# Normalisations on both sides of the linear attention in batches of four tiles, and the fifth unit's final product ahead of one

## The reference, cut to what matters

```python
h = h + soft_moe(layernorm(h))                # its last product is added to h
x = layernorm(h)                              # normalised once
g = ln(x) * ln1_w + ln1_b                     # and again
k, v = g @ Wk_a.T, g @ Wv_a.T
sr = sigmoid(g @ Wr_a.T)
y = bi_wkv(decay / T, first / T, k, v)        # (ef*af + eb*ab + ec*v) / (ef*bf + eb*bb + ec)
x = x + sr * y @ Wo_a.T
g = ln(x) * ln2_w + ln2_b
kf = square(relu(g @ Wk_f.T))
x = x + sigmoid(g @ Wr_f.T) * (kf @ Wv_f.T)
```

## Time and profile before

| | |
|---|---|
| median of 3 runs | 1508.24 us (1503.82 to 1509.28) |
| profiled execution | 1508.46 us, span 1506.7 us |
| mean granted clock of TensorE | 0.952 |
| busy: TensorE matmul, weight load | 1324.3 us (88%), 763.3 us (51%) |
| busy: DVE, ACT, POOL | 911.4 us (60%), 673.4 us (45%), 553.1 us (37%) |

### The profile page before, as it was taken

The page is one execution under the profiler, slowest core; times in us unless marked ns, Lnnn a source line. Parts: engine busy times, 40 slices in busy tenths (PEclk is TensorE's granted clock), DMA queues, the critical chain, the costliest instruction groups (busy, mean ns, idle before and its releaser), DMA issues.

```text
span 1506.7 us, 18440 instructions
## 1 busy us (share of the span) xinstructions
PE 1324.3 (88%) x6684; PEld 763.3 (51%) x6684; DVE 911.4 (60%) x1509; ACT 673.4 (45%) x1210; POOL 553.1 (37%) x399
## 2 busy tenths in 40 slices
PE   7978889898989867389988869979999999999998
PEld 6634445454545434254433444558756668444444
DVE  4789999999999999862100168846446614121022
ACT  4776767677777744152100027631452241313311
POOL 1477898988989887300000010012044202000000
PEclk9989999999999999779999979999999999899999
DMA  6404051422414040437999920000000001020101
GB/s 205 172 2 171 13 162 35 138 76 96 128 45 171 12 161 0 187 129 265 399 391 400 328 70 1 1 0 1 22 17 2 1 1 38 0 110 14 37 0 33
DMA packets 38773, 151.96 MB, mean 101 GB/s; under 512 B 10364, under 2 KB 14587, under 8 KB 33948
## 3 DMA queue, kind: packets, MB, share of 16 engines
q1 hardware_dynamic: 34588, 149.21, 27.5%
q10 hardware_dynamic: 4096, 1.58, 0.4%
HBM read 147.56 MB, written 1.63 MB: 99 GB/s over the span
## 4 chain that ended last, share of the span: by engine, by line
PE 51%; DVE 20%; issue 11%; ACT 6%; POOL 6%; DMA 5%; SPq 1%; ACTq 0%; DVEq 0%; POOLq 0%
PE ps L1915 49%; DVE arena L1508 7%; DVE arena L1497 5%; DMA arena<-in_e_b 4%; POOL arena L824 4%; ACT arena L926 2%; ACT ps L1037 1%; DVE stats L1392 1%; DVE arena L1798 1%; PE ps L1924 1%; SPq L636 1%; ACT arena L931 1%; DVE arena L1517 1%; POOL arena L835 1%; POOL arena L839 1%
## 5 line engine op out<-in xcount | busy, mean ns | idle before, releaser
L1915 PE MATMUL ps<-arena 64*32 64x384 f32 (+17 forms) x5236 | 948.6, 416 | 100.2 <-ACT arena L926 22.4
L1915 PEld LDWEIGHTS ps<-arena 64*32 64x32 f32 (+15 forms) x5236 | 537.3, 154 | 483.0 <-issue 288.6
L824 POOL TENSOR_TENSOR arena<-arena 128x784 f32<-128x784 f32 x192 | 367.4, 1927 | 95.3 <-DVE arena L1508 94.7
L1915 PE MATMUL ps<-arena,ident 128*128 128x392 f32 x900 | 348.3, 515 | 50.9 <-POOL arena L824 42.7
L1508 DVE TENSOR_TENSOR_SCAN arena<-ps,arena 128x784 f32<-128x784 f32 x192 | 341.0, 1776 | 2.4 <-ACT ps L1037 2.4
L1915 PEld LDWEIGHTS ps<-arena,ident 128*128 128x128 f32 x900 | 169.1, 195 | 199.2 <-POOL arena L824 74.2
L1037 ACT ACTIVATE ps<-arena 128x384 f32<-128x384 f32 x384 | 207.9, 575 | 115.8 <-DVE arena L1508 115.1
L926 ACT ACTIVATE arena<-ps 128x392 f32<-128x392 f32 (+9 forms) x269 | 126.7, 489 | 284.7 <-PE ps L1915 203.4
L926 ACT ACTIVATE arena<-ps,arena 128x392 f32<-128x392 f32 (+2 forms) x191 | 103.4, 602 | 229.6 <-PE ps L1915 144.8
L1497 DVE TENSOR_TENSOR arena<-ps,arena 128x784 f32<-128x784 f32 x192 | 182.7, 952 | 6.0 <-ACT ps L1063 4.8
L1661 DVE COPY arena<-ps 128x384 f32<-128x384 f32 x32 | 16.3, 552 | 152.5 <-PE ps L2169 152.5
(11 more groups left out here) (201 smaller groups left out, 854.6 us busy)
## 6 DMA issues: line engine op xcount, KB each, us to landing
arena<-in_e_w SPq DMA_DIRECT2D x32, 2304.0 KB
arena<-bc_rows SPq DMA_DIRECT2D x128, 392.0 KB, 4.7
arena<-in_patches SPq DMA_DIRECT2D x4, 1176.0 KB, 7.5
arena<-comb_rows SPq DMA_DIRECT2D x1, 3136.0 KB, 10.7
arena<-in_mlp_w SPq DMA_DIRECT2D x5, 576.0 KB, 4.3
arena<-arena ACTq DMA_DIRECT2D x128, 12.0 KB, 8.2
arena<-in_mlp_w SPq DMA_DIRECT2D x5, 384.0 KB, 3.4
arena<-in_mlp_w SPq DMA_DIRECT2D x10, 192.0 KB, 3.9
```

The costliest lines, as they stand in the source:

```text
L824: pool.tensor_tensor(pair(hbuf[:, at % SLOTS, :]), pair(hbuf[:, at % SLOTS, :]), c_all[:, n:n + 2, :], ALU.mult).then_inc(times_c, 1)
L1915: return pe.matmul(dst, lhsT, rhs, start=first, stop=last)
```

## The change

The eight tiles of the first half are normalised in two batches of four at both borders, with the turns, the copies and the products split to match: one batch feeds one quarter. At the first border the second half (batch of eight, `mixed(range(4, 8))`) moves behind `front(0)`, and its turn behind `arguments(0)`. At the second border `final(4)` stands ahead of `attended`. The banks are given out anew. The amount of matrix and activation work is the same; DVE gets one more chain of small instructions at each border.

```diff
-        s_mix = items("mix", 8, "dve")
+        s_mix = stage("mix", "dve")
+        plan(s_mix, 8, (0, 1, 2, 3, 5, 6, 7, 0), "dve")
...
-        plan(s_xaT, 4, (0, 1, 2, 3), "act")
-        plan(s_kvr, 6, (0, 1, 2, 3), "act")
-        plan(s_xaT, 4, (4, 5, 6, 7), "act")
+        plan(s_xaT, 2, (1, 2), "act")
+        plan(s_kvr, 3, (3, 1, 2), "act")
+        plan(s_xaT, 2, (3, 1), "act")
+        plan(s_kvr, 3, (2, 3, 1), "act")
...
+            if t == 0:
+                plan(s_xaT, 4, (5, 6, 7, 0), "act")
...
-        plan(s_xbT, 4, (0, 1, 2, 3), "act")
-        plan(s_rf, 4, (4, 5, 6, 7), "act")
-        plan(s_kf, 12, range(8), "act")
+        plan(s_xbT, 2, (2, 3), "act")
+        plan(s_rf, 2, (4, 0), "act")
+        plan(s_kf, 6, (1, 7, 2, 3, 4, 0), "act")
+        plan(s_xbT, 2, (1, 7), "act")
+        plan(s_rf, 2, (2, 3), "act")
+        plan(s_kf, 6, (4, 0, 1, 7, 5, 6), "act")
...
@@ ScalarE
-            turned_in(s_xaT, range(4), 0)
+            turned_in(s_xaT, range(2), 0)
             kvr_out(0)
+            turned_in(s_xaT, range(2, 4), 0)
             kvr_out(1)
-            turned_in(s_xaT, range(4, 8), 0)
             for t in range(7):
                 if t < 6:
                     exps(t)
+                if t == 0:
+                    turned_in(s_xaT, range(4, 8), 0)
...
-            for k in range(2):
-                turned_in(s_xbT, range(4 * k, 4 * k + 4), 2)
-                for i in range(4 * k, 4 * k + 4):
+            for tiles in (range(0, 2), range(2, 4), range(4, 8)):
+                k = tiles.start // 4
+                turned_in(s_xbT, tiles, 2)
+                for i in tiles:
...
-                for i in range(12 * k, 12 * k + 12):
+                for i in range(3 * tiles.start, 3 * tiles.stop):
...
@@ VectorE
-            def twice_normed(src, again, k, ready, signal):
+            def twice_normed(src, again, tiles, ready, signal):
...
-            for k in range(2):
-                for i in range(4 * k, 4 * k + 4):
+            def mixed(some):
+
+                for i in some:
                     s_mix.wait_filled(dve, i)
                     TT(two_tiles(h, i), two_tiles(h, i), pair_of(s_mix, i), ALU.add).then_inc(s_mix.taken["dve"], 1)
-                twice_normed(h, xa, k, lambda i: s_mix.wait_taken(dve, i // 2), xa_ready)
+                twice_normed(h, xa, range(2 * some.start, 2 * some.stop), lambda i: s_mix.wait_taken(dve, i // 2),
+                             xa_ready)
+
+            mixed(range(0, 2))
+            mixed(range(2, 4))
...
-            def attended(k):
-
-                dve.wait_ge(normed_once, 8 * k + 8)
-                for i in range(4 * k, 4 * k + 4):
+            def attended(some):
+
+                tiles = range(2 * some.start, 2 * some.stop)
+                dve.wait_ge(normed_once, tiles.stop)
+                for i in some:
...
             for t in range(8):
                 if t < 6:
                     front(t)
+                if t == 0:
+                    mixed(range(4, 8))
                 if 1 <= t <= 6:
                     back(t - 1)
-                if t == 6:
-                    attended(0)
                 if t >= 2:
                     final(t - 2)
+                if t == 6:
+                    attended(range(0, 2))
+                    attended(range(2, 4))
             squares(0)
-            attended(1)
+            attended(range(4, 8))
...
@@ TensorE
-            turn(s_xaT, xa, xa_ready, 0)
+            turn(s_xaT, xa, xa_ready, range(2))
             kvr_in(0)
+            turn(s_xaT, xa, xa_ready, range(2, 4))
             kvr_in(1)
-            turn(s_xaT, xa, xa_ready, 1)
             pe.wait_ge(const_ready, MIX_CONST + 1)
             for t in range(7):
                 if t < 6:
                     arguments(t)
+                if t == 0:
+                    turn(s_xaT, xa, xa_ready, range(4, 8))
...
-            turn(s_xbT, xa, xb_ready, 0)
-            receptance(0)
-            channel_hidden(0)
+            for q in range(2):
+                turn(s_xbT, xa, xb_ready, range(2 * q, 2 * q + 2))
+                receptance(range(2 * q, 2 * q + 2))
+                channel_hidden(range(6 * q, 6 * q + 6))
             wkv_out(1)
             channel_out(0)
-            turn(s_xbT, xa, xb_ready, 1)
-            receptance(1)
-            channel_hidden(1)
+            turn(s_xbT, xa, xb_ready, range(4, 8))
+            receptance(range(4, 8))
+            channel_hidden(range(12, 24))
```

More of the change, by code:

```diff
@@ L1408, in normalise @@
                           ALU.subtract, ALU.mult)
-            def twice_normed(src, again, k, ready, signal):
-                ks = slice(8 * k, 8 * k + 8)
-                norm_stats(src, range(8 * k, 8 * k + 8), ready, (1.0 + LN_EPS, LN_EPS * LN_EPS))
+            def twice_normed(src, again, tiles, ready, signal):
+                ks = slice(tiles.start, tiles.stop)
+                norm_stats(src, tiles, ready, (1.0 + LN_EPS, LN_EPS * LN_EPS))
                 own.then(STT(nmean[:, ks], mv[:, ks, 0], -1.0, rs[:, 0, ks], ALU.mult, ALU.mult))
-                for i in range(8 * k, 8 * k + 8):
+                for i in tiles:
                     normalise(again, src, i, rs[:, 1, :]).then_inc(signal, 1)
@@ L1731, in final @@
                     .then_inc(s_sum.taken["dve"], 1)
-            def attended(k):
-                dve.wait_ge(normed_once, 8 * k + 8)
-                for i in range(4 * k, 4 * k + 4):
+            def attended(some):
+                tiles = range(2 * some.start, 2 * some.stop)
+                dve.wait_ge(normed_once, tiles.stop)
+                for i in some:
                     s_wo4.wait_filled(dve, i)
                     TT(two_tiles(x1, i), two_tiles(x1, i), pair_of(s_wo4, i), ALU.add).then_inc(s_wo4.taken["dve"], 1)
-                norm_stats(x1, range(8 * k, 8 * k + 8), lambda i: s_wo4.wait_taken(dve, i // 2))
-                for i in range(8 * k, 8 * k + 8):
+                norm_stats(x1, tiles, lambda i: s_wo4.wait_taken(dve, i // 2))
+                for i in tiles:
                     normalise(xa, x1, i, rstd).then_inc(xb_ready, 1)
@@ L1763, in _ @@
                     front(t)
+                if t == 0:
+                    mixed(range(4, 8))
                 if 1 <= t <= 6:
                     back(t - 1)
-                if t == 6:
-                    attended(0)
                 if t >= 2:
                     final(t - 2)
+                if t == 6:
+                    attended(range(0, 2))
+                    attended(range(2, 4))
             squares(0)
-            attended(1)
+            attended(range(4, 8))
             gated_sum(0)
-            twice_normed(h, xb_, 0, lambda i: s_vf.wait_taken(dve, i // 2), x5_ready)
+            twice_normed(h, xb_, range(8), lambda i: s_vf.wait_taken(dve, i // 2), x5_ready)
             squares(1)
             gated_sum(1)
-            twice_normed(h, xb_, 1, lambda i: s_vf.wait_taken(dve, i // 2), x5_ready)
+            twice_normed(h, xb_, range(8, NT), lambda i: s_vf.wait_taken(dve, i // 2), x5_ready)
             dve.wait_ge(normed_once, 2 * NT)
@@ L2271, in wkv_out, with receptance @@
                     ins.then_inc(s_wo4.filled, 1)
-            def receptance(k):
-                for i in range(4 * k, 4 * k + 4):
+            def receptance(tiles):
+                for i in tiles:
                     s_xbT.wait_taken(pe, 2 * (i // 2) + 1)
@@ L2282, in receptance, with channel_hidden @@
                     ins.then_inc(s_rf.filled, 1)
-            def channel_hidden(k):
-                for i in range(12 * k, 12 * k + 12):
+            def channel_hidden(some):
+                for i in some:
                     q, m = divmod(i, 6)
@@ L2304, in channel_out, with turn @@
                     ins.then_inc(s_vf.filled, 1)
-            def turn(s, src, ready, k):
-                transposed(s, src, lambda i: pe.wait_ge(ready, i + 1), some=range(4 * k, 4 * k + 4))
+            def turn(s, src, ready, some):
+                transposed(s, src, lambda i: pe.wait_ge(ready, i + 1), some=some)
             pe.wait_ge(loaded["rw"], 16 * RW_LOADS)
             pe.wait_ge(loaded["rwB"], 16 * 6)
-            turn(s_xaT, xa, xa_ready, 0)
+            turn(s_xaT, xa, xa_ready, range(2))
             kvr_in(0)
+            turn(s_xaT, xa, xa_ready, range(2, 4))
             kvr_in(1)
-            turn(s_xaT, xa, xa_ready, 1)
             pe.wait_ge(const_ready, MIX_CONST + 1)
@@ L2324, in _ @@
                     wkv_out(0)
-            turn(s_xbT, xa, xb_ready, 0)
-            receptance(0)
-            channel_hidden(0)
+            for q in range(2):
+                turn(s_xbT, xa, xb_ready, range(2 * q, 2 * q + 2))
+                receptance(range(2 * q, 2 * q + 2))
+                channel_hidden(range(6 * q, 6 * q + 6))
             wkv_out(1)
             channel_out(0)
-            turn(s_xbT, xa, xb_ready, 1)
-            receptance(1)
-            channel_hidden(1)
```

(7 more changed lines are left out.)

## The result

The changed kernel takes **1502.1 us** (median of 20 runs, 1497.6 to 1509.05), the kernel before beside it 1508.36 (20 runs, 1503.82 to 1511.07): a ratio of 0.9967, 95% interval 0.9956 to 0.9979, so 5.0 us faster (3.2 to 6.6); the medians stand 6.3 apart. The forecast was 1502.7, range 1499.0 to 1507.0, with 0.70 on a difference under 0.5%. Time and sign came out as forecast. The sum was 0.9 for the head and 4.6 for the tail; what follows tests whether each is where it was put. The profiled execution of after took 1506.11 us (span 1504.4, granted clock 0.955), so it is one of the slower ones; that of before has span 1506.7.

What follows compares the result with a forecast made beforehand. TensorE was taken as the bound, so gains come only from its waits, breaks beside transposes and clock. Head 0.9 plus tail 4.6 make 5.5 us off the 1508.24 median: 1502.7 us, range 1499.0 to 1507.0.

Steps and rivals of the forecast that it cites:

- the head: First border: normalising four tiles first starts `kvr_in(0)` 4.2 us earlier, mostly given back; 0.9 us gained.
- the tail: Second border: `receptance` starts 8.05 us earlier, less 1.84 and 1.6; 4.6 us gained, 6.2 or 2.9 by clock.
- The wait for `final(4)` goes: Tail: the second half of unit 5's sums runs without a wait, and `receptance` begins at 994.4, not 1002.45.
- The tail gives back 1.84 and 1.6: Tail: a second turn of two groups costs 1.84 us, one slow stretch behind the 991.4 to 994.4 break 1.6.
- Each needs the other: Tail: smaller batch alone still waits on `final(4)`; moving `final(4)` alone leaves TensorE waiting for a tile at 993.
- one stretch costing 1.7 and a start of `kvr_in(2)` at 907.85: Head: 3.4 us at 1.2 GHz in `kvr_in(0)` costs 1.7; `kvr_in(2)` begins at 907.85, before at 908.7.
- Small instructions: DVE's chains ahead of the first normalised tile: thirteen instructions take 2.77 us in the head, eleven 2.4 in the tail.
- Banks: Head: second transposes wait for bank 2 until 885.6; a mix-bank wait over 1 us would show the prediction wrong.
- the held clock (1500.1): Rival: the clock holds behind both breaks, 1.9 + 6.2 = 8.1 us gained; held in one or both, chance 0.26.
- Head gives nothing: Rival: bank, DVE or a longer slow stretch eats the head's 0.9; tail alone, 1503.6 to 1504.4; chance 0.18.
- The slower one (four long stretches): Rival: each of four breaks starts a 6.8 us half-clock stretch, 13.6 against 8.1: 5.5 slower, 1513.7; chance 0.05.
- slow stretches elsewhere are my guess: Whole kernel: a guess at why runs of before spread over 1503.8 to 1509.3, which the prediction couldn't assign.

Runs made afterwards that it cites:

- e3: Kernel before with only `final(4)` moved ahead of the normalisation of all eight tiles: 1503.48 us, ratio 0.9973.
- e4: Kernel before with the tail's two batches of four and split turns, but `final(4)` not moved: 1511.41 us, ratio 1.0016.
- e1: Kernel before with the tail part of the change alone, head as before: 1502.64 us, ratio 0.9957 to before.
- e9: The changed kernel measured and profiled again with no edit: 1502.21 us, ratio 0.9966 to the kernel before.
- e10: Changed kernel with products that nothing reads put only in the later feed-forward stage, 1262 to 1332 us: 1495.31 us, ratio 0.9919 to before.
- e8: Kernel before with `final(4)` moved, plus products that nothing reads in its two remaining breaks: 1501.70 us, ratio 0.9962.
- e6: Changed kernel with products that nothing reads in its head and tail breaks: 1499.82 us, ratio 0.9953 to before.
- e12: Kernel before with products that nothing reads put only in the later feed-forward stage: 1500.81 us, ratio 0.9954.
- e2: Kernel before with the head part of the change alone, tail as before: 1504.53 us, ratio 0.9976 to before.
- e7: Changed kernel with both the reordering of e5 and the fillers of e6, some cut or left out: 1498.36 us, ratio 0.9936 to before.
- e5: Changed kernel with banks reordered ahead of `kvr_in(2)` and the tail's second turn placed between products: 1500.33 us, ratio 0.9949 to before.

## Why the prediction was right, and where not

- *The wait for `final(4)` goes*: right, shown by e3 (the move alone takes the wait away) and e4 (without it 6.9 us are left). `receptance` came 8.1 earlier against `sums(5)`, forecast 8.05; DVE's first tile had 3 us to spare, and ACT's reciprocal decides the start, as written. The next ACTIVATE begins 1.30 behind the start of its table load (993.34 to 994.64). The Trainium skill (ScalarE: Activation LUTs, What ACT_TABLE_LOAD costs) has 2.66 for a switch; this trace does not agree, as the earlier trace rows did not.
- *The tail gives back 1.84 and 1.6*: right. The second break is 1.87, and the stretch at 998.1 costs 1.7. Tail measured 4.5 in after and e1. The likeliest case is not the only one: tails of 56.9 (e9) and 53.7 (e10, the clock held) occur too, 3.0 to 6.2 gained, the very bounds given (2.9 and 6.2). The lower one is right by luck: it was to come from a stretch behind each turn, and came from one of 6.8 us behind the first.
- *"Each needs the other"*: **wrong**. The step that failed is the one that lets TensorE "wait for a tile at 993" as if that cost the gain. It waits 2.2 us in e3, but its one turn of eight tiles hides its copies (`receptance` follows at once, 997.39) and needs no second turn. With the clock held e8 and e6 are equal, 53.4 and 53.7.
- *Head, one stretch costing 1.7 and a start of `kvr_in(2)` at 907.85*: the term was mis-sized for the first profile, which has the head 3.5 us longer than forecast. The stretch behind the first wait was 6.8 us long in both kernels; before, `kvr_in` stood in only its last 3.6, now in 5.8 of it, so 2.9 went where 1.7 was put. And the turn ahead of `kvr_in(2)` was priced as a wait for ACT, not as a break that can lose the clock: 3.1 long, another 1.7. The Trainium skill (TensorE: Matmul & The Clock Gate, Part 4: PE-mode transpose) says that transposes do not count as busy for the clock; by that its sixteen are part of the break, and the fall at 909.4 agrees, though behind the same break in e9 the clock held. The prediction weighed this for two breaks and not for this one. The profiled head is 2.6 slower. Over four profiles with the batches (113.5, 110.6, 110.6, 109.1) the mean is 111.0, over five without (110.9, 111.7, 111.4, 110.9, 111.5) 111.3: a gain of 0.3 where 0.9 stood. Nine profiles of a part that varies by 4 us tell neither from the other nor from none, so that the time came out within 0.6 us is partly luck. What differs is how long the clock is lost behind the first wait: without the batches for 6.8 us (before, e4, e12) or 10.2 (e1, e3), with them for 6.8 (after), 3.4 (e9, e10) or not at all (e2).
- *Small instructions*: the chain counted as thirteen is fourteen (884.80 to 887.57), the one of the tail twelve and not eleven; the sums stand, since the times 2.77 and 2.4 are right.
- *Banks*: right. The wait on the mix banks is 0.17 us, DVE is not late at `kvr_in(2)`.
- *Rivals*: the held clock (1500.1) does occur in parts, in the head of e2 and in the tail of e10; no profile without fillers has both. "Head gives nothing" is not excluded: e1, with the head as before, has 1502.6, the changed kernel 1502.1, and the 0.8 to 6.3 us of e2 can come from the later stage. The slower one (four long stretches) was never seen, three stretches at most. The 5.5 us of e12 against e10 are the forecast's sum to the tenth, which is partly luck, since a head worth less and a tail of varying worth make it up.
- *Spread of before, "slow stretches elsewhere are my guess"*: shown for the larger part, and placed at 1262 to 1332 us by e9 and e10 for the changed kernel and by e12 for the one before.

Open: whether the two parts alone add up to more than the whole, as their medians say and their intervals leave open. Seven of the changed kernel's twenty runs lie below 1499.1, so the later stage may hold its clock more often in one program than in another, which would do it; the two parts were not tried with that stage filled.

## What to carry to other kernels

When a wait goes, look at what each batch edit around it adds by itself: here moving one instruction pair had the whole gain of the tail at a given clock, and the finer batches there paid for themselves only once their extra turn stood between products. A break that holds only transposes and copies is priced twice, as time and as clock behind it, and a product that starts earlier behind a break can run more of its work at 1.2 GHz. Where runs spread by more than the change is worth, find the stretch that spreads, hold its clock with products that nothing reads, and compare again.

## What was not expected of the hardware

- The clock fell or held behind the same break in different executions: behind 885 us for 6.8 us (after), 3.4 (e9) or not at all (e2), with the same order of instructions in that part. Without the batches it fell there in all five profiles, for 6.8 or 10.2 us (885.2 to 895.4 in e1). Breaks of 3.1 us with eight or sixteen transposes in them are where it goes either way (at 909 in after, not in e9).
- Fillers of 0.3 to 2 us a break, 6.6 us in all (an estimate from their widths, at 0.66 us for 392 columns), were enough for 1.00 over 207 us. Where the clock holds by itself they cost 0.2 to 0.3 us (head 109.3 in e6 and 109.1 in e2, 108.4 in e7 and 108.1 in e5).
- A chain of small DVE instructions costs about the same at any width: 0.20 us apart on 98x4 (988.21 to 989.98, nine of them) as on 98x16 (0.21).
